# Two products of a pair made by turns in two PSUM banks, in a quantised convolution block

## What is computed

```python
residual = x
out = conv3x3_decomposed(x, lsq_quantize(w1, alpha1))
out = jax.nn.relu(batchnorm(out, gamma1, beta1))
out = conv3x3_decomposed(out, lsq_quantize(w2, alpha2))
out = batchnorm(out, gamma2, beta2)
out = jax.nn.relu(out + residual)
```

## Time and profile before

| what | value |
|---|---|
| runs before | 1503.12, 1502.04, 1502.94 us; median 1502.94 |
| the profiled execution's own time | 1499.78 us |
| its span, from the first to the last instruction | 1497.7 us |
| mean granted TensorE clock over the span | 0.888 |
| busy: PE, DVE, ACT, POOL | 1133.3, 1126.5, 854.2, 296.5 us |
| TensorE's first product of phase 1, last matmul of phase 2 | about 24 and 1178 us from the span's start |

### The profile page before, as it was taken

The page is one execution under the profiler, slowest core; times in us unless marked ns, Lnnn a source line. Parts: engine busy times, 40 slices in busy tenths (PEclk is TensorE's granted clock), DMA queues, the critical chain, the costliest instruction groups (busy, mean ns, idle before and its releaser), DMA issues.

```text
span 1497.7 us, 19193 instructions
## 1 busy us (share of the span) xinstructions
PE 1133.3 (76%) x5802; PEld 1030.2 (69%) x5802; DVE 1126.5 (75%) x1624; ACT 854.2 (57%) x1261; POOL 296.5 (20%) x147
## 2 busy tenths in 40 slices
PE   3999999999999998699999999999999400000000
PEld 2998999999999998599999999999999400000000
DVE  7998888888888885898888888888887552222322
ACT  3556555656655555677777777777776552122222
POOL 3232222222222221222222222222222000000000
PEclk9999999999999999799999999999999755555555
DMA  4354454444452210022255544444232599999998
GB/s 165 155 190 163 183 199 181 172 172 172 188 198 86 86 43 0 1 86 86 109 190 193 194 172 172 172 181 162 86 129 72 211 429 430 432 429 430 431 430 352
DMA packets 27813, 296.88 MB, mean 198 GB/s; under 512 B 3856, under 2 KB 3856, under 8 KB 4240
## 3 DMA queue, kind: packets, MB, share of 16 engines
q1 hardware_dynamic: 22608, 245.25, 41.7%
q10 hardware_dynamic: 5184, 51.38, 8.1%
HBM read 174.59 MB, written 122.03 MB: 198 GB/s over the span
## 4 chain that ended last, share of the span: by engine, by line
issue 66%; POOL 13%; another core or an unknown queue 11%; DVE 5%; DMA 4%; POOLq 1%; ACT 0%; DVEq 0%; SPq 0%
POOL v_lo L409 13%; DVE slots L810 4%; DMA slots<-conv_spill 3%; DMA out<-slots 1%; ACT slots L565 0%; POOLq L414 0%; DVEq L810 0%; POOLq L408 0%; POOLq L77 0%; DVEq L808 0%; POOLq L409 0%; DVEq L264 0%; DVE affine L743 0%; DVE tiny L741 0%
## 5 line engine op out<-in xcount | busy, mean ns | idle before, releaser
L409 POOL TENSOR_TENSOR v_lo<-v_rows,v_hi 128x1008 fp32r<-128x1008 f32 x128 | 294.2, 2318 | 831.7 <-ACT v_hi L448 831.7
L865 PE MATMUL conv_psum<-d_hi,w2T 128*128 128x398 f32 (+2 forms) x864 | 284.7, 333 | 0.1
L865 PE MATMUL conv_psum<-d_hi,w1T 128*128 128x398 f32 (+2 forms) x864 | 284.6, 333 | 0.0
L865 PE MATMUL conv_psum<-d_lo,w1T 128*128 128x398 f32 (+2 forms) x864 | 283.3, 332 | 0.0
L865 PE MATMUL conv_psum<-d_lo,w2T 128*128 128x398 f32 (+2 forms) x864 | 283.3, 332 | 0.0
L810 DVE SCALAR_TENSOR_TENSOR slots<-slots,affine,xbuf 128x3136 f32 (+1 forms) x32 | 110.9, 3483 | 192.2 <-DMA slots<-conv_spill 187.7
L845 PE MATMUL conv_psum<-v_hi,w2T 128*128 128x512 f32 x576 | 227.7, 395 | 18.3 <-DVE v_lo L636 18.3
L845 PE MATMUL conv_psum<-v_hi,w1T 128*128 128x512 f32 x576 | 228.3, 396 | 10.1 <-DVE v_lo L636 5.5
L479 ACT ACTIVATE squares<-slots,minus_shift 128x1008 bf16 (+3 forms) x192 | 225.0, 1172 | 7.1
L845 PE MATMUL conv_psum<-v_lo,w1T 128*128 128x512 f32 x576 | 228.5, 397 | 0.0
L845 PE MATMUL conv_psum<-v_lo,w2T 128*128 128x512 f32 x576 | 228.0, 396 | 0.0
(11 more groups left out here) (74 smaller groups left out, 1490.4 us busy)
## 6 DMA issues: line engine op xcount, KB each, us to landing
conv_spill<-slots SPq DMA_DIRECT2D x44, 1568.0 KB, 6.1
slots<-conv_spill SPq DMA_DIRECT2D x44, 1568.0 KB, 21.0
xbuf<-in_x SPq DMA_DIRECT2D x32, 1568.0 KB, 56.4
out<-slots ACTq DMA_DIRECT2D x32, 1568.0 KB, 11.7
slots<-in_x SPq DMA_DIRECT2D x31, 1568.0 KB, 8.9
slots<-in_L_conv_w SPq DMA_DIRECT2D x2, 576.0 KB, 9.8
slots<-in_x SPq DMA_DIRECT2D x1, 1036.0 KB, 8.4
slots<-in_x SPq DMA_DIRECT2D x1, 532.0 KB, 9.3
```

Source lines behind the costliest of these rows:

```text
L409: nc.gpsimd.tensor_tensor(pair_window(1, k), pair_rows(k), pair_window(0, k).bitcast(F32), ALU.subtract).then_inc(pool_lo_ready, 1)
L865: last = nc.tensor.matmul(bank_run(CHUNK_BANK[j], r1 - r0), w[:, kh * 3 + kw, :], run(d_plane[half], r0 - WINO + 1, r1 - WINO + 1, kw - 1) ...
```

## The change

The loop over the six products becomes a loop over three pairs. Inside a pair the matmuls alternate: column tap 0 with the high part for the first product, the same for the second product, then the low part for both, and so on, so that consecutive matmuls go to two banks by turns and use different weight slices. `m_done` is still raised once for each product, at its own last matmul, which is now the eleventh and the twelfth of a pair's twelve, and was the sixth and the twelfth. The waits are drawn together at the head of the pair.

```diff
-                for k in range(M):
-                    if k == 0:
+                for pair in range(PAIRS):
+                    if pair == 0:
                         pe.wait_ge(lo_ready, g * LO + 1)
-                        if not first_step:
+                    else:
+                        pe.wait_ge(pool_lo_ready, g * PLO + pair)
+                    if not first_step:
+
+                        if pair == 0:
                             pe.wait_ge(m_copied, g * 2 - 1)
-                    if k == 2:
-                        pe.wait_ge(pool_lo_ready, g * PLO + 1)
-                    if k == 4:
-                        pe.wait_ge(pool_lo_ready, g * PLO + 2)
-                    if not first_step:
-
-                        if k in (1, 2, 3):
-                            pe.wait_ge(sums_ready, g * SR - (0, 4, 1, 0)[k])
-                        if k in (4, 5):
-                            pe.wait_ge(rows_ready, g * RR - (k - 4))
+                            pe.wait_ge(sums_ready, g * SR - 4)
+                        if pair == 1:
+                            pe.wait_ge(sums_ready, g * SR)
+                        if pair == 2:
+                            pe.wait_ge(rows_ready, g * RR)
+
                     for kw in range(3):
                         for half in range(2):
-                            last = nc.tensor.matmul(bank_run(M_BANK[k], TILES),
...
-                    last.then_inc(m_done, 1)
+                            for k in (2 * pair, 2 * pair + 1):
+                                last = nc.tensor.matmul(bank_run(M_BANK[k], TILES),
...
+                                if kw == 2 and half == 1:
+                                    last.then_inc(m_done, 1)
```

More of the change, by code:

```diff
@@ L843, in products @@
                     for kw in range(3):
                         for half in range(2):
-                            last = nc.tensor.matmul(bank_run(M_BANK[k], TILES),
-                                                    w[:, M_WEIGHT[k] + kw, :],
-                                                    run(v_plane[half], k * TILES, (k + 1) * TILES, kw - 1),
-                                                    start=(kw == 0 and half == 0), stop=(kw == 2 and half == 1))
-                    last.then_inc(m_done, 1)
+                            for k in (2 * pair, 2 * pair + 1):
+                                last = nc.tensor.matmul(bank_run(M_BANK[k], TILES),
+                                                        w[:, M_WEIGHT[k] + kw, :],
+                                                        run(v_plane[half], k * TILES, (k + 1) * TILES, kw - 1),
+                                                        start=(kw == 0 and half == 0), stop=(kw == 2 and half == 1))
+                                if kw == 2 and half == 1:
+                                    last.then_inc(m_done, 1)
```

## The result

| | before | after |
|---|---|---|
| median of the runs | 1502.49 us (4 runs) | 1512.18 us (4 runs) |
| lowest and highest | 1501.32, 1503.12 | 1512.12, 1512.31 |
| ratio, 95% interval | | 1.0067 [1.0055, 1.0079] |
| the profiled execution: time, span | 1499.78, 1497.7 | 1512.12, 1510.2 |

The changed kernel is slower by 9.7 us between the medians, or 0.6%, and the interval of the ratio leaves out 1. 1511.9 was forecast, in a range of 1505 to 1518. (One more run of before joined the three shown ahead, so its median is now 1502.49.)

A forecast was written before the change was run, and what follows sets the result against it. TensorE was taken to set the pace up to about 1178 us, before a transfer-bound tail of some 320 us. Median 1502.94 + 9.0 of phase 2 stalls, all other terms 0, gave 1511.9 us; range 1505 to 1518.

The forecast's parts named there:

- When m3 is complete: Product 2's last matmul comes five places, 1.16 us, later, and ScalarE's waiting copy of m3 is delayed by all of it.
- The copy of m1: ScalarE's copy of product 0 moves from 881.07 to about 881.9 us, a shift contained in that of m3's copy.
- The chain behind it and the slack of 0.83 us: Phase 2: ScalarE works 9.51 us unbroken to chunk 0's read-out, which now ends 0.33 us too late for chunk 2's load.
- 0.31 us for each stall, 29 of them: TensorE waits at chunk 2 in phase 2's steps 1 to 29, 9.0 us in all; chance 0.76.
- its own stall: Phase 2's first step already has a stall of 0.42 us at chunk 2, which was to stay.
- Phase 1 free: Without ReLU, ScalarE's 1.70 us of idle time before chunk 0 takes up the 1.16 us delay; cost 0.
- Pace 0: Product matmul intervals stay at 0.232 us despite bank changes; cost 0, bounds -4.6 to +4.6 us.
- VectorE and GpSimd hidden: Their work moves about 1.1 us later, covered by VectorE's 2.16 us idle before `lo_direct` and early low parts; cost 0.
- The median: Forecast for the median of the runs: 1502.94 + 9.0 = 1511.9 us, 0.6% slower.
- The clock: Rival: TensorE's clock falls to half, product intervals 0.42 instead of 0.232 us, 1936 us in all; chance 0.01.
- The rule on rotating banks: Skill's rule: rotate independent groups through banks so read-out overlaps matmuls; turns give that up within a pair, loss size unstated.

The follow-up runs named there:

- experiments 2 and 3: experiment 2, and the changed kernel with only the second pair whole (1506.64 us) or only the second pair by turns (1511.60 us).
- experiment 5: Changed kernel with one bank for eleven of a pair's twelve matmuls, one product's weight slices, or one input per pair: 1511.21, 1510.83, 1507.93 us.
- experiment 1: Changed kernel, but in phase 2 ScalarE reads out chunk 0 between the two ReLU activations instead of after both: 1503.15 us.
- n = 3: Kernel before, products whole, ScalarE's copy of m3 waiting for product 3's third matmul, 0.70 us later: 1502.11 us.
- experiment 2: Kernel before, products whole, ScalarE's copy of m3 delayed by 0.70, 0.93, 1.16 or 1.39 us: 1502.11, 1503.99, 1511.26, 1517.48 us.
- n = 6: Kernel before, products whole, ScalarE's copy of m3 waiting for product 3 to be complete, 1.39 us later: 1517.48 us.
- one-bank variant: Changed kernel with eleven of a pair's twelve matmuls in its first bank, only the last in the second; results spoilt: 1511.21 us.

## Why the prediction was right, point by point

- **When m3 is complete.** Five intervals, 1.16 us, later: shown by experiments 2 and 3. The copy of m1 was also late, and its delay was contained in the other, as said: with only the second pair by turns m1 is as early as before, and 8.6 us are lost all the same.
- **The chain behind it and the slack of 0.83 us.** The chain from the copy of m3 to the end of chunk 0's read-out took 9.52 us, and 9.51 was forecast. The threshold lies between 0.70 and 0.93 us of delay.
- **0.31 us for each stall, 29 of them.** 9.1 us measured for 9.0, 29 waits in the trace. The price taken from phase 2's first step, where the stall already existed, held. That this first step would keep its own stall did not: in the profile of the changed kernel the distance there is 0.35 us, as without a stall, though the step is no shorter. Nothing in the sum hung on it.
- **Phase 1 free.** No stall there at 0.70 to 1.39 us of delay. ScalarE's idle time before chunk 0, 1.70 us in the earlier trace rows, fell to 0.53, and about 0.5 was forecast. This is the same place in the changed kernel, and then the row of ScalarE's waits for the two chunks of a step in 200 to 560 us, which was 91.7 us in all before:

```profile
311.14 0.50 ACT L467 ACTIVATE slots<-conv_psum 128x392 f32 x1 [0.53 <-PE conv_psum L867]
...
ACT slots L467 <- PE conv_psum L867: 64.6, 41, 2.7
```

- **Pace 0.** Not quite: +0.013 us a step, 0.85 us in all, inside the bounds of 4.6 either way, and I had written that any move of phase 1's period would count against the term. By that sign the term was wrong, though small. The reason given was half right. Bank and weight slice cost nothing in this order, which experiment 5 shows directly, but the step of the argument that read "what it alters for each is its predecessor" listed only these two. The order also decides which input follows which.
- **VectorE and GpSimd hidden.** VectorE's idle time before `lo_direct` fell from 2.16 to 1.31 us in a step of phase 2; 1.0 to 1.4 was forecast. Experiment 1 shows that it costs nothing.
- **The median.** That it came within 0.3 us of the forecast is partly luck. The forecast started from 1502.94 us, the median of three runs, and four gave 1502.49; it added 9.0, and 9.7 were measured, against 9.1 + 0.85 by the steps. The two errors have opposite signs, and the runs of one kernel spread by some 4 us (below).
- **The clock.** From 37.4 to 600 us and from 621 to 1194 us of the changed kernel the granted clock stayed 1.00; it was at the lower level in part of the very first step and between the phases. The windows view of the changed kernel, one window in each phase (us; PE, PEld, DVE, ACT, POOL busy; granted clock; DMA share; GB/s):

```profile
200.00:300.00 100.00, 100.00 (x518) 91.63 (x517) 87.86 (x139) 58.23 (x102) 26.45 (x12) 1.00 0.51 193
...
900.00:1000.00 100.00, 99.66 (x504) 88.74 (x503) 86.26 (x134) 73.16 (x113) 23.80 (x11) 1.00 0.47 179
```

- **The rule on rotating banks** (the Trainium skill, Perfetto Trace Analysis, the section on optimizing TensorE performance): the runs agree with its reason, the overlap of read-out and matmuls, and say what it is worth here. It is nothing as long as the reader's slack covers the delay (0.0 us at n = 3), and 9.1 us where it doesn't. No version that computes the whole result was clearly faster than the kernel before: the turns had no gain to set against the loss.

## What to carry to other kernels

When an order is changed inside a group, ask first when each result of the group is complete, and follow the engine that waits for it to the next thing that it releases. The loss is the delay less the slack at that release, times the steps in which the chain is unbroken; here the two were 0.3 us apart, and phase 1, with 3.3 us less work on ScalarE, lost nothing. If such an order is wanted for another reason, moving one short read-out ahead of a longer operation on the engine that is waited for takes the loss away, as in experiment 1.

## What the runs showed of the hardware that was not expected

**A matmul's interval depends on the order of its inputs.** With the same 90 matmuls and weight loads in a step, the period of phase 1 was 17.567, 17.580, 17.593 or 17.627 us by the order of the 36 product matmuls alone, and the same to 0.001 us in all kernels with one order. Two orders share 17.567: whole products, and only the second pair by turns. In phase 1 it did not matter when the other engines worked: the four kernels of experiment 2 move ScalarE and VectorE by 0.7 to 1.4 us, and each keeps the 17.567 of before. In phase 2 it was not quite so: with n = 6 the products took 8.371 instead of 8.344 us in 5 of the 29 steps, though their order is that of before, where none did. Of bank, weight slice and input, each changed alone in the order of the full turns, only the input changed the period. By what rule was not found.

**The first steps differ from profile to profile by more than the pace.** The first product matmul is at 24.06 in the profile before and at 24.07 after, but the first chunk matmul at 37.41 before,

```profile
37.41 0.35 PE L865 MATMUL conv_psum<-d_hi,w1T 128*128 128x398 f32 x1
```

and at 39.98 after:

```profile
39.98 0.35 PE L867 MATMUL conv_psum<-d_hi,w1T 128*128 128x398 f32 x1
```

The windows view of the changed kernel shows why, in the columns after POOL's:

```profile
27.00:30.50 3.50, 1.48 (x6) 0.86 (x5) 2.69 (x4) 0.58 (x1) 3.50 (x1) 1.00 0.00 0
30.50:37.00 6.50, 5.24 (x12) 4.12 (x13) 5.19 (x5) 0.14 (x1) 3.30 (x2) 0.50 0.00 0
```

TensorE paused for GpSimd's low part (until 31.76), the clock fell to its lower level, 1.2 GHz, and twelve matmuls ran with about 0.43 us between them. In the profile before, the matmuls were still 0.43 us apart when the same wait began, the clock rose during it, at about 30 us, and stayed at 2.4 GHz after it:

```profile
30.50:37.00 6.50, 5.25 (x23) 4.31 (x24) 5.21 (x5) 2.55 (x3) 4.21 (x3) 1.00 0.00 0
```

This is not the change: the kernel of n = 3, whose products are whole, also had its first chunk matmul late, at 40.18, and the one-bank variant, with turns, had it at 37.41. In six of the other profiles (n = 3 among them) the clock also fell after a second pause, of 3.9 us, that began between 116 and 120 us, and that step took 19.0 to 19.3 us instead of 17.7. From the first product matmul to step 6 the thirteen profiles differ by 4.2 us, 114.3 to 118.5; before has the shortest and the changed kernel 116.9. The difference between these two, 2.6 us, is part of the 12.5 between the profiled spans, and the 4.2 us fit the spread of the runs of before, 1499.76 to 1504.18 us in 23 of them. Had the forecast been checked by the two profiled times alone, the loss would have seemed 12.3 us.
